# The q/k/v projection of an adaLN transformer layer: unrolled, its products in f16 high and low parts, its work dealt over four engines

## The reference, cut to what matters

```python
h = _layernorm(x, axis=-1) * (1 + ca) + sa
...
q = split_heads(x @ Wq + bq)
k = split_heads(x @ Wk + bk)
v = split_heads(x @ Wv + bv)
scores = jnp.einsum('bhid,bhjd->bhij', q, k)
```

## Time and profile before

| what | value |
|---|---|
| median of 3 runs | 3905.11 us (3901.54 to 3906.79) |
| profiled execution, its own time | 3913.09 us |
| span of the profiled execution | 3911.5 us |
| PE busy | 3411.8 us (87%) |
| DVE busy | 2384.1 us (61%) |
| ACT busy | 1407.0 us (36%) |
| POOL busy | 1270.0 us (32%) |
| first matmul of the first projection iteration | 59.15 us from the span's start |
| first instruction of the attention phase | 264.27 us |

### The profile page before, as it was taken

How to read it: one execution, slowest core, us unless ns; L and a number is a source line. 1 busy time by engine, 2 the same in 40 slices (tenths; PEclk the granted TensorE clock), 3 DMA queues, 4 the chain that set the end, 5 groups by cost and what they waited for, 6 DMA issues and landing times. The chain is left out here.

```text
span 3911.5 us, 164368 instructions
## 1 busy us (share of the span) xinstructions
PE 3411.8 (87%) x72480; PEld 2951.2 (75%) x72480; DVE 2384.1 (61%) x4876; ACT 1407.0 (36%) x1690; POOL 1270.0 (32%) x1501
## 2 busy tenths in 40 slices
PE   6964999999989999999899999989999999189980
PEld 4534888888878888888788888878888888168770
DVE  5853567777256666753566777346567771276774
ACT  1320233344512334354123334522233446155551
POOL 1004433222354332234443322344333211222556
PEclk8986999999989999999899999999999999599995
DMA  3764101000311010003111000131000000544664
GB/s 112 207 169 115 34 24 35 28 26 19 91 55 41 29 37 26 19 29 109 37 39 37 29 19 26 45 97 35 29 29 29 22 13 11 176 128 141 191 181 131
DMA packets 249778, 259.11 MB, mean 66 GB/s; under 512 B 104041, under 2 KB 192333, under 8 KB 248957
## 3 DMA queue, kind: packets, MB, share of 16 engines
q1 hardware_dynamic: 227964, 205.30, 17.9%
q0 software_dynamic: 21120, 43.42, 3.6%
HBM read 151.36 MB, written 95.99 MB: 63 GB/s over the span
## 5 line engine op out<-in xcount | busy, mean ns | idle before, releaser
L887 DVE TENSOR_TENSOR att_acc<-att_pm,att_acc 128x512 f32<-128x512 f32 x1920 | 1267.1, 687 | 542.0 <-PE att_pm L1006 265.3
L967 ACT ACTIVATE att_pt<-att_ps 128x1024 f32<-128x1024 f32 x560 | 573.7, 1025 | 1611.9 <-PE att_ps L998 1603.3
L998 PE MATMUL att_ps<-att_qz,table_z 128*128 128x64 f16 x8960 | 729.7, 194 | 8.9 <-issue 8.8
L995 PE MATMUL att_ps<-att_qx,table_x 68*128 68x64 f16 x8960 | 732.1, 195 | 4.7 <-issue 4.6
L970 ACT ACTIVATE att_pt<-att_ps 128x1024 f32<-128x1024 f32 x528 | 515.3, 1022 | 354.1 <-PE att_ps L1006 351.9
L998 PEld LDWEIGHTS att_ps<-att_qz,table_z 128*128 128x128 f16 x8960 | 621.8, 99 | 8.9 <-issue 8.7
L995 PEld LDWEIGHTS att_ps<-att_qx,table_x 68*128 68x128 f16 x8960 | 619.3, 99 | 8.2 <-issue 7.9
L1088 PE MATMUL att_po<-att_pt,att_vn 128*32 128x128 f32 x17408 | 603.3, 280 | 1.8 <-issue 1.6
L991 PE MATMUL att_ps<-att_qs,att_kn 113*128 113x64 f16 x8960 | 455.5, 194 | 76.5 <-DMA att_qs<-s_m 71.3
L1088 PEld LDWEIGHTS att_po<-att_pt,att_vn 128*32 128x32 f32 x17408 | 452.1, 111 | 88.5 <-issue 73.1
L991 PE MATMUL att_pm<-att_qs,att_kn 113*128 113x64 f16 x8672 | 444.9, 195 | 81.3 <-POOL att_qx L759 46.9
(11 more groups left out here) (209 smaller groups left out, 4073.8 us busy)
## 6 DMA issues: line engine op xcount, KB each, us to landing
att_qe<-s_q SPq DMA_DIRECT2D x256, 128.0 KB
moe_xs<-s_h SPq DMA_DIRECT2D x78, 256.0 KB
s_y<-moe_y SPq DMA_DIRECT2D x78, 256.0 KB
s_v<-prj_vx SPq DMA_DIRECT2D x32, 512.0 KB, 3.9
att_vn<-s_v SPq DMA_DIRECT2D x64, 256.0 KB, 3.5
att_qs<-s_q SPq DMA_DIRECT2D x128, 66.0 KB
prj_x<-in_x POOLq DMA_DIRECT2D x16, 512.0 KB, 4.3
att_kn<-s_k SPq DMA_DIRECT2D x128, 64.0 KB, 2.5
```

The costliest lines, as they stand in the source:

```text
L887: dve.tensor_tensor(held, got, held, ALU.max).then_inc(bank_done, 1)
L967: act.activation(pt[:, k % 2, :, t * 64:t * 64 + 64].rearrange("p h (x c) -> p x h c", x=2), ps[t][:, :, :].rearrange("p x (h c) -> p x h ...
L995: last = pe.matmul(groups[:, :, g], keep["table_x"][:, y:y + P], qx[0:G * D + G, s, x * (XQ // G) + g], start=False, stop=(g == XQ // G - ...
L998: last = pe.matmul(groups[:, :, g], keep["table_z"][:, y:y + P], qz[:, s, x * (XQ // G) + g], start=False, stop=(g == XQ // G - 1), skip_g ...
```

## The change

- The loops are unrolled into straight programs; addresses that came from registers are constants, and `mod_now`, the copy of the batch entry's shift and scale, is gone.
- The three weight matrices are split once, at the start, into f16 high parts (ACT) and f16 low parts (DVE); PE's first transpose comes after this.
- The transposed, modulated input is written in f32 (hf, ACT), then cast to an f16 high part (ACT), and its f16 low part is made by POOL (`low_input`, 1024 elements a partition). PE's qp products wait for that.
- Each f32 product becomes three f16 products: high times high, low weight times high input, high weight times low input. A qp tile has six matmuls of 512 columns, a v tile six of 256 columns for each 128 tokens. The transposes stay f32.
- The move of qp out of PSUM with the bias (qf) goes from DVE to ACT, and the four low parts `lo` of an iteration go from DVE to POOL. POOL's order in an iteration is low 0, load of x for two iterations on, low 1, low 2, low_input of the following iteration, low 3.
- ACT's order is qf 0, hi 0, square root, qf 1, hi 1, qf 2, hi 2, hf and high part of the following iteration, qf 3, hi 3. DVE's is the norm of the following iteration, then vx.

```diff
+                def low_input(it):
+                    s, u = it % 2, it // 2
+                    pool.wait_ge(h_hi[s], u + 1)
+                    pool.tensor_tensor(hs[:, s, 1], hf[:, s], hs[:, s, 0], ALU.subtract).then_inc(h_lo[s], 1)
+                def low(it, n):
+                    pool.wait_ge(hi_done[n], it + 1)
+                    if it:
+                        pool.wait_ge(lo_out[n], it * 16)
+                    pool.tensor_tensor(lo[:, n, :], qf[:, n, :], hi[:, n, :], ALU.subtract).then_inc(lo_done[n], 1)
...
+                load_x(0)
+                load_x(1)
+                low_input(0)
+                for it in range(NK):
+                    for n in range(4):
+                        if n == 3 and it + 1 < NK:
+                            low_input(it + 1)
+                        low(it, n)
+                        if n == 0 and it + 2 < NK:
+                            load_x(it + 2)
...
                 def main(b, c, it, following):
-                    for n in range(4):
-                        dve.wait_ge(qp_done[n], it + 1)
...
-                        dve.tensor_scalar(qf[:, n, :], qp[n][:, :], bias, None, ALU.add).then_inc(qf_done[n], 1)
-                        if n:
-                            low(it, n - 1)
-                        elif following:
-                            ahead(*following)
-                    low(it, 3)
+                    if following:
+                        ahead(*following)
...
+                for n, w in enumerate((wq, wk, wv)):
+                    dve.wait_ge(w_hi, n + 1)
+                    dve.tensor_tensor(ws[:, n, 1], w[:, :, :], ws[:, n, 0], ALU.subtract).then_inc(w_split, 1)
...
+                        last = act.activation(hf[:, s, eh, :], tp[eh][:, :], ACT.Identity,
+                                              bias=keep["shift_a"][:, eh, b:b + 1],
+                                              scale=keep["scale_a"][:, eh, b:b + 1])
                     last.then_inc(hT_done[s], 1)
+                    act.wait_ge(hT_done[s], u + 1)
+                    act.activation(hs[:, s, 0], hf[:, s], ACT.Copy).then_inc(h_hi[s], 1)
...
                 def split(it, n):
+                    act.wait_ge(qp_done[n], it + 1)
...
+                    act.activation(qf[:, n, :], qp[n][:, :], ACT.Identity, bias=bias).then_inc(qf_done[n], 1)
                     act.wait_ge(qf_done[n], it + 1)
                     act.activation(hi[:, n, :], qf[:, n, :], ACT.Copy).then_inc(hi_done[n], 1)
...
-                    pe.wait_ge(hT_done[s], u + 1)
+                    pe.wait_ge(h_lo[s], u + 1)
                     for n in range(4):
...
+                        for pw, ph in PARTS:
+                            for eh in range(EH):
+                                last = pe.matmul(qp[n][:, :], ws[:, n // 2, pw, eh, (n % 2) * P:(n % 2 + 1) * P], hs[:, s, ph, eh, :],
+                                                 start=(pw == ph == eh == 0), stop=(ph == 1 and eh == EH - 1))
```

More of the change, by code:

```diff
@@ L258, in phase_project @@
         tick = a.sb("tick", [P, 1])
-        mod_now = a.sb("mod_now", [P, 2, EH])
         mv = a.sb("mv", [P, 2, JT, 2])
@@ L283, in phase_project, with order @@
         NK = B * CPB
[L285 to L292, removed]
+        def order(ahead, main):
             ahead(0, 0, 0)
-            with eng.Fori(0, B - 1) as b:
-                batch(b, False)
-            batch(B - 1, True)
+            for it in range(NK):
+                main(it // CPB, it % CPB, it, ((it + 1) // CPB, (it + 1) % CPB, it + 1) if it + 1 < NK else None)
         slot_use = lambda b, c: b * (CPB // 2) + c // 2
@@ L402, in main @@
                         root(*following)
-                    for n in range(1, 4):
-                        split(it, n)
+                    split(it, 1)
+                    split(it, 2)
                     if following:
-                        act.wait_ge(vp_done[1], it)
                         modulate(*following)
-                order(act, ahead, main)
+                    split(it, 3)
+                act.wait_ge(weights, 48)
+                for n, w in enumerate((wq, wk, wv)):
+                    act.activation(ws[:, n, 0], w[:, :, :], ACT.Copy).then_inc(w_hi, 1)
+                act.wait_ge(once, 1)
+                order(ahead, main)
             @block.tensor
             def _(pe):
-                pe.wait_ge(weights, 48)
+                pe.wait_ge(w_split, 3)
+                PARTS = ((0, 0), (1, 0), (0, 1))
                 def ahead(b, c, it):
@@ L425, in main @@
                     s, u = c % 2, slot_use(b, c)
-                    pe.wait_ge(hT_done[s], u + 1)
+                    pe.wait_ge(h_lo[s], u + 1)
                     for n in range(4):
[L428 to L432, removed]
+                        if it:
+                            pe.wait_ge(qf_done[n], it)
+                        for pw, ph in PARTS:
+                            for eh in range(EH):
+                                last = pe.matmul(qp[n][:, :], ws[:, n // 2, pw, eh, (n % 2) * P:(n % 2 + 1) * P], hs[:, s, ph, eh, :],
+                                                 start=(pw == ph == eh == 0), stop=(ph == 1 and eh == EH - 1))
                         last.then_inc(qp_done[n], 1)
@@ L436, in main @@
                     for n in range(2):
-                        pe.wait_ge(vx_done[n], it)
+                        if it:
+                            pe.wait_ge(vx_done[n], it)
                         for j in range(2):
-                            for eh in range(EH):
-                                last = pe.matmul(vp[n][:, j, :], hT[:, s, eh, (2 * n + j) * P:(2 * n + j + 1) * P],
-                                                 wv[:, eh, :], start=(eh == 0), stop=(eh == EH - 1))
+                            for pw, ph in PARTS:
+                                for eh in range(EH):
+                                    last = pe.matmul(vp[n][:, j, :], hs[:, s, ph, eh, (2 * n + j) * P:(2 * n + j + 1) * P],
+                                                     ws[:, 2, pw, eh, :], start=(pw == ph == eh == 0), stop=(ph == 1 and eh == EH - 1))
                         last.then_inc(vp_done[n], 1)
-                order(pe, ahead, main)
+                order(ahead, main)
             @block.sync
@@ L448, in _ @@
                 sp.dma_start(io["s_q"][:, :, 2 * D].rearrange("b u h t -> (b u) (h t)"), nought[:, :]).then_inc(nought_out, 16)
-                with sp.Fori(0, NK) as it:
+                for it in range(NK):
                     for n in range(4):
```

48 lines of the change are left out of this document (24 added, 24 removed).

## The result

The changed kernel takes 3936.76 us (median of 4 runs, 3932.53 to 3942.82) against 3903.32 us (3899.88 to 3906.79) of the kernel before: **+33.4 us**, a ratio of 1.008, 95% interval 1.0064 to 1.0097. The prediction said slower and +22, 3927 us; the time lies inside its range, outside the forecast's own 3920 to 3934.

The account below looks back on a forecast made before the run. It took a loop of PE, DVE's queue and ACT to bound the projection at 12.52 us per iteration. Periods +20.6, start +3.6 and end -2.3 gave +22: 3905 + 22 = 3927 us, range 3893 to 3945, forecast's own 3920 to 3934.

Parts of the forecast that it names:

- chain from xn to the next qp: Per iteration, transposes, hf, high part and low_input between xn's end and the next qp matmul: 6.0 us, with v covered.
- The second small step: DVE's inverse-root step L240, due at 3.35 us after the first qp, held by POOL's low 0 until about 4.25.
- The start: Before the first qp: weight subtractions on DVE +0.3, high part 1.1 and low_input 2.25 on the way; +3.6 us.
- What POOL does to it: POOL's low parts hold DVE's second small step and two xn instructions; xn ends at 7.9 us instead of 6.1.
- The clock: Rival: granted clock falls in PE's waits, doubling first qp tile and transposes; up to 36 us more, 3945 to 3963; chance 0.13.
- The end: After the last qp began, v follows directly: 9.6 us instead of 11.9 until the last v store is issued; -2.3 us.
- the 1.3 added for a slow first one: In the period sum, 1.3 us added to 15 x 13.9 for the slow-clock first period (13.86 - 12.52).
- Not held: Rival: POOL does not hold xn at all on DVE; period 12.1, total -4 us, 3901; chance 0.17.
- Held once: Rival: POOL holds xn on DVE once, not twice; xn ends at 7.1, period 13.1, +10 us, 3915; chance 0.18.
- an instruction with one SBUF source too: Step generalising from a held DVE cast: DVE waits for the whole POOL instruction even with one SBUF source.
- faster: Rival: neither small steps nor xn held on DVE; period 11.3, -17 us, 3888, decisive under about 12.0; chance 0.10.

Follow-up runs that it names:

- x_load_on_sp: Changed kernel with only the issue of the x loads moved from POOL to SP; 3924.3 us against 3906.1 before, ratio 1.0044.
- redeal_only: Changed kernel with its products left in f32, without high and low input and weight parts, unrolling and dealing kept; 3907.6 us against 3908.8 before.
- pe_kept_busy: Changed kernel plus 24 unused matmuls per iteration on PE, twelve in front of each of its two waits; 3941.1 us against 3906.1 before.
- root_before_low0: Changed kernel with statistics taken two iterations ahead and the square root before qf 0, arithmetic on the same engines; 3900.8 us against 3908.8 before.
- no_refinement: Changed kernel without the three small steps that refine the inverse root, the plain reciprocal used instead; 3920.1 us, single run.
- norm_ahead_low_pool: norm_ahead with the low parts of q and k on POOL again, as in the changed kernel; 3887.9 us against 3905.2 before.
- lo_on_dve: Changed kernel with the four low parts back on DVE, POOL keeping only low_input and x loads; 3901.3 us against 3906.1 before.
- norm_ahead_f32: norm_ahead with its products left in f32, no high and low parts of input and weights, no low_input; 3887.5 us against 3905.2 before.
- norm_ahead: Changed kernel with norm two iterations ahead, next input transposed before this qp, low parts on DVE; 3861.8 us against 3908.8 before.

## Why the prediction was right, and by how much it was off

**Direction and mechanism.** PE's cheaper products lie beside the path; xn, hf, the high part and low_input lie on it. The forecast's chain from xn to the next qp was 6.0 us and measured 5.99 (low_input 2.13 of 2.15, the high part 1.06 of 1.06, hf 1.45 of 1.43 and the transposes 1.10 of 1.10). The second small step was held 0.91 us to 198.74, 4.10 after the iteration's start, where 4.25 was forecast. The start was +3.5 of +3.6, though not only for the reasons given: the statistics began at 49.91 instead of 51.2, and a table load of 1.28 us on ACT now stood in front of the first square root.

**The step that was mis-sized** is *What POOL does to it*: "xn is four instructions ... two are done by then, the third is held until 6.4, the fourth by low 2 until about 7.6. xn ends at 7.9". The prediction let the third small step through during the x load, as that reads no tile. In the trace it was issued 0.31 us into the x load and held until low 1 and low 2 had both ended; xn ended at 8.53. That is 0.62 us per period, 9.3 us over fifteen. x_load_on_sp shows that the x load's place in POOL's queue matters: with it on SP 7.8 and 13.77.

What tells the cases apart is whether low 1 was ready, that is whether hi 1 was done. In the changed kernel hi 1 is done at 198.82, before L244 is issued (198.98); in redeal_only it is done at 128.51 (the cast of 0.63 from 127.88), after L244 (128.28), and L244 passes beside the same x load in 0.16 us. In the changed kernel's own iteration at 76.66 it is done at 82.19, after L244 (81.10), and L244 passes too. This holds without an exception in the traces of the five kernels that keep the x load between low 0 and low 1 (changed, pe_kept_busy, redeal_only, root_before_low0, no_refinement). Of the small steps and xn instructions issued during such an x load, 36 came after hi 1 was done, by 0.02 us at the least, and each was held until low 2 had ended, 2.78 to 3.10 us; 103 came before hi 1 was done, and none took over 0.48. So the x load itself holds nothing; a low part that is ready behind it does, before the profile shows it start. Why DVE gets no turn between low 1 and low 2 in this case, as it does in norm_ahead_low_pool, stays open.

The Trainium skill, page Perfetto Trace Analysis, section GPSIMD Engine Instruction, says that spans on GpSimd in a profile are unreliable, and that the start-to-start spacing is to be used. The rows above agree: DVE was held 0.47 us before the profile's start of low 1.

**The clock** had 0.13 as a rival with +36 if it fell in each iteration. It fell in twelve of the fifteen, but over the transposes in seven only, otherwise over v, where it is covered, or over qp in the first two, whose periods came out shorter: 5.2 us. It belonged into the forecast as a part, not beside it as a case. **The end** was to give back 2.3 us and gave 0.2: the last qp ran at half clock in part (6.99 instead of 5.35 us, 1.6 of the 2.1 that are missing), and from the end of the last v store's issue to attention 4.61 us passed instead of 4.01.

Sum by measured terms: 9.3 + 5.2 in the periods, less 2.9 for three that were shorter (12.90, 13.78, 14.01) and the 1.3 added for a slow first one, is 10.3 on the forecast's 20.6, which gives the 30.9. With 2.1 less given back at the end and 0.1 less at the start, the forecast's 22 become the measured 34 between the marks.

**The rivals.** "Not held" fell. "Held once" is what the first two iterations show (xn's last instruction alone, 1.25 and 1.30 us), where the slow clock made hi 1 late; in the twelve that make up the bulk L244 and not xn is held. The step from the cast to "an instruction with one SBUF source too" went too far: the reciprocal (L238), which has one SBUF source as well, is never held (below). The Trainium skill, page SBUF — State Buffer, section Who interferes with whom, was cited for tensor_scalar, of which no row before showed a hold; now the trace agrees: one xn instruction took up to 1.347 us in the changed kernel, against 0.414 at most before. The "faster" case needed a period under 12.0. root_before_low0 is that case made true by the order: 11.05, where 11.3 was computed, and then the clock took back 1.7 of it in four iterations and a late xn 2.1 to 2.8 in three others, so that 3901 came out and not 3888.

**What each part of the change is worth**, from the runs: unrolling 0; the dealing alone 0 (the wait for hT is gone, and one for xn, which DVE's holds make late, has come); the f16 products with the unrolling +37 in the old dealing. Together they cost 33. Of the orders that were run, the f16 products gain (26 us) only in the one in which PE hardly waits.

## What to carry to other kernels

Making an engine's work cheaper moves the end only if that engine, and not a chain through the others, sets the period: here the same products cost 37 us in one order and gained 26 in another. Before arithmetic is moved to POOL, look which DVE instructions will run beside it, and of which kind they are; small ones on the path can cost their neighbour's whole duration, and a chain that is a full iteration ahead only helps while DVE's queue has room. When a phase stops being compute bound, count PE's waits too: here waits of about 2 us in each iteration came with half-clock stretches.

## What the runs showed of the hardware that was not expected

- A DVE instruction of 128x4 elements took 2.78 us instead of 0.16 when it was issued during a POOL x load with one low part ready behind it and a second soon after; with the x load moved to SP it took 1.10. When the low part was not ready yet, it took 0.16 beside the same x load.
- Which DVE instructions POOL's subtractions held depends on their kind. In the eleven kernels of this case with such subtractions, of the projection's instructions on DVE that were issued while one of them ran, at least 0.3 us before its end, all of these took longer than alone: L240 and low parts (tensor_tensor, both sources in SBUF), L242 and L244 (scalar_tensor_tensor), xn and the small addition of epsilon (tensor_scalar, one SBUF source). None of these did: 94 reciprocals (0.18 at most), 262 statistics over 256 elements (0.43), 259 aggregations (0.18) and 174 parts of vx (0.43), which read one source from PSUM.
- In lo_on_dve the clock fell to 1.2 GHz in about every second iteration, though PE was busy for 135 of 165 us and waited once for 2.21 us and otherwise for 0.25 at most; with no wait (norm_ahead_f32, 75 to 200 us), with waits of 0.93 at most (norm_ahead to 190 us) and with one of 1.10 in each iteration (redeal_only, 75 to 240) it was 1.00. The price depends on what follows the wait: 1.7 us where it was qp, 0.87 where it was the transposes, nothing where it was v.
- The table load of 1.28 us stood on ACT at 39.47 before, far ahead of the first square root; with the weights' casts put in between it came at 52.01, on the path.
